# Gathers of batch n+2 between the scatters of batch n in the first layer's sums

## What is computed

```python
def spmm(edge_row, edge_col, edge_val, m):
    gathered = edge_val[:, None] * m[edge_col]
    return jax.ops.segment_sum(gathered, edge_row, num_segments=N_NODES)
h = spmm(edge_row, edge_col, edge_val, x @ W1)
h = jax.nn.relu(h)
out = spmm(edge_row, edge_col, edge_val, h @ W2)
...
x = _layernorm(x + _L0_gnn_ref(x, src, dst, edge_weight, L0_gnn_W1, L0_gnn_W2), axis=-1)
```

## Time and profile before

| what | value |
|---|---|
| median of 3 runs | 11682.42 us (11674.79 to 11685.21) |
| the profiled execution | 11694.18 us, its span 11692.3 us |
| mean granted TensorE clock of the span | 0.728 |
| PE busy, share of the span | 7181.3 us, 61% |
| PEld (weight loads) busy | 6410.3 us, 55% |
| VectorE (DVE) busy | 5776.1 us, 49% |
| ScalarE (ACT) busy | 2434.9 us, 21% |
| POOL busy | 6563.8 us, 56% |
| first and last gather (L1107) begin | 945.0 us, 4218.3 us |

### The profile page before, as it was taken

One profiled execution on the slowest core, in us unless ns is written; L12 is line 12 of the kernel. 1 busy time (PEld: TensorE's weight loads), 2 busy tenths in 40 slices (PEclk: granted clock), 3 DMA queues, 4 the chain that ended last, 5 costly groups with the idle time before them and its releaser, 6 DMA issues. The chain is left out here.

```text
span 11692.3 us, 252242 instructions
## 1 busy us (share of the span) xinstructions
PE 7181.3 (61%) x80158; PEld 6410.3 (55%) x80186; DVE 5776.1 (49%) x20072; ACT 2434.9 (21%) x6859; POOL 6563.8 (56%) x6504
## 2 busy tenths in 40 slices
PE   5877999977999966333333633333332466666663
PEld 5867998856988953333333433333331355555552
DVE  7985666635666663111111242222225466666665
ACT  3552222222222222000000000000001233333332
POOL 1324555524555523777777227777773377777771
PEclk8888999998999977555555565555555666666665
DMA  1015555545555544111111111111112111111113
GB/s 37 0 35 126 134 133 130 133 105 129 132 132 131 131 135 164 52 53 52 52 53 52 49 48 52 52 52 53 52 52 62 48 49 49 50 49 49 49 50 57
DMA packets 760187, 884.18 MB, mean 76 GB/s; under 512 B 136806, under 2 KB 645583, under 8 KB 760015
## 3 DMA queue, kind: packets, MB, share of 16 engines
q0 software_dynamic: 203776, 424.26, 15.7%
q1 hardware_dynamic: 555880, 452.87, 13.4%
q10 hardware_dynamic: 487, 6.55, 0.2%
HBM read 766.26 MB, written 123.29 MB: 76 GB/s over the span
## 5 line engine op out<-in xcount | busy, mean ns | idle before, releaser
L521 PE MATMUL psum<-sel,ring 128*128 128x128 f32 x6272 | 1451.3, 426 | 2533.6 <-DMA ring<-hyp_table,idx 1268.2
L521 PEld LDWEIGHTS psum<-sel,ring 128*128 128x128 f32 x6272 | 1356.3, 329 | 2629.2 <-issue 2629.2
L456 POOL DMA_INDIRECT ring<-att_table,idx x1592 | 1762.3, 1107 | 501.8 <-issue 472.1
L456 POOL DMA_INDIRECT ring<-hyp_table,idx x1568 | 1487.4, 949 | 487.2 <-issue 477.6
L456 POOL DMA_INDIRECT ring<-rel_table,idx x1568 | 1484.3, 947 | 487.0 <-issue 477.3
L508 DVE TENSOR_TENSOR acc<-acc,psum 128x128 f32 x392 | 113.1, 289 | 3075.2 <-PE psum L521 3075.2
L1107 PE MATMUL psum<-state,ring 128*128 128x128 bf16 x24420 | 1517.9, 221 | 40.8 <-DVE ring L1054 34.6
L1061 DVE TENSOR_SCALAR state<-iota_row,state 128x128 f32<-128x128 f32 x5684 | 1527.9, 346 | 0.0
L1107 PEld LDWEIGHTS psum<-state,ring 128*128 128x128 bf16 x24420 | 1380.0, 98 | 150.3 <-issue 51.5
L1040 POOL DMA_INDIRECT ring<-gcn_table,idx x812 | 781.3, 962 | 748.4 <-ACT idx L1085 624.7
L1040 POOL DMA_INDIRECT ring<-rows,idx x812 | 780.4, 961 | 742.3 <-ACT idx L1085 618.4
(11 more groups left out here) (353 smaller groups left out, 11153.5 us busy)
## 6 DMA issues: line engine op xcount, KB each, us to landing
state<-xparts SPq DMA_DIRECT2D x814, 192.0 KB
state<-drow SPq DMA_DIRECT2D x814, 160.0 KB
rel_table<-tout SPq DMA_DIRECT2D x98, 512.0 KB, 2.6
ring<-rows SPq DMA_DIRECT2D x70, 448.0 KB
ring<-att_table,idx POOLq DMA_INDIRECT x1592
ring<-rel_table,idx POOLq DMA_INDIRECT x1568
ring<-hyp_table,idx POOLq DMA_INDIRECT x1568
rows<-acc SPq DMA_DIRECT2D x42, 448.0 KB
```

Of the source, the lines that this page charges most:

```text
L456: pool.indirect_dma_start(out=ring[:, u, k, 0:width], out_offset=None, in_=table, in_offset=bass.IndirectOffsetOnAxis(ap=idx[:, u, k:k + 1 ...
L521: last = nc.tensor.matmul(psum[:, u % 2, 0:WIN], ring[:, u, k, 0:D], sel[:, u % 2, k, :], start=(k == 0), stop=(k == K - 1))
```

## The change

TensorE's loop body becomes one function, `step`. Where `gather` of batch n+1 with its 30 products stood ahead of `scatter` of batch n, the products that gather cell j of batch **n+2** now stand ahead of the scatters of cell j of batch n, for j = 0 to 4; cells 5 and 6 have scatters alone. Since n+2 and n have the same v, the buffers of a step are those of one parity. All the waits of the gathers, and that for `picked`, stand at the head of the step. VectorE makes the slots of n+2 ahead of the sources of n, and batches 0 and 1 are gathered ahead of the loop; SP loads one more batch at the end, whose gathers nobody uses. CT, the size of the table of places, stays the same number.

```diff
--- before.py
+++ after.py
@@ -49,7 +49,7 @@
 GB = -(-(-(-E // P)) // GC)
 assert GB % 2 == 0 and (GB + 1) * GC <= EC and AW * SW <= NPAD and AW <= P
 CELLS = SG * GB * SJ
-CT = -(-(CELLS + SJ) // P)
+CT = -(-(CELLS + 2 * SJ) // P)
 BC = SJ * P
 PC = JP * P
 TOP = TILES * P - SW
@@ -1025,9 +1025,11 @@
                         with sp.Fori(0, GB // 2) as it:
                             for v in range(2):
                                 load(sg * GB + it * 2 + v, it * 2 + v, v)
-                    load(LAST, GB, 0)
-                    sp.wait_ge(sem("xin0"), (LAST // 2 + 1) * 16)
-                    sp.wait_ge(sem("din0"), (LAST // 2 + 1) * 16)
+                    for v in range(2):
+                        load(LAST + v, GB, v)
+                    for v in range(2):
+                        sp.wait_ge(sem(f"xin{v}"), (LAST // 2 + 1) * 16)
+                        sp.wait_ge(sem(f"din{v}"), (LAST // 2 + 1) * 16)
 
                 @block.gpsimd
                 def _(pool):
@@ -1064,12 +1066,13 @@
                         ins.then_inc(sem("picked"), 1)
 
                     nc.vector.memset(zeros_b, 0.0).then_inc(sem("sent"), 1)
-                    to_slots(0, 0, 16)
+                    for v in range(2):
+                        to_slots(v, v, 16)
                     with dve.Fori(0, SG) as sg:
                         with dve.Fori(0, GB // 2) as it:
                             for v in range(2):
                                 n = sg * GB + it * 2 + v
-                                to_slots(n + 1, 1 - v, sg * (GB * 8) + it * 16 + (16 + 16 * v))
+                                to_slots(n + 2, v, sg * (GB * 8) + it * 16 + 32)
                                 to_sources(n, v)
                         dve.wait_ge(sem("closed"), sg + 1)
                         win = acc[:, bass.ds(sg * SUMS, SUMS)].rearrange("p (j h s) -> p j h s", h=2, s=P)
@@ -1097,23 +1100,28 @@
 
                 @block.tensor
                 def _(pe):
-                    def gather(n, v, loaded):
+                    def may_gather(n, v, loaded):
                         pe.wait_ge(sem("reach"), n + 3)
                         pe.wait_ge(sem(f"xin{v}"), loaded)
                         pe.wait_ge(sem("got"), n + 1)
-                        for j in range(JP):
-                            for t in range(2):
-                                for i in range(3):
-                                    last = nc.tensor.matmul(rowsP[v][:, j * P:(j + 1) * P],
-                                                            reach[v][:, t, j * P:(j + 1) * P],
-                                                            xwin[v][:, t, i, :],
-                                                            start=(t + i == 0), stop=(t + i == 3))
-                        last.then_inc(sem("gat"), 1)
-
-                    def scatter(n, v, fetches):
-                        pe.wait_ge(sem("got"), n + 3)
+
+                    def gather(v, j):
+                        for t in range(2):
+                            for i in range(3):
+                                last = nc.tensor.matmul(rowsP[v][:, j * P:(j + 1) * P],
+                                                        reach[v][:, t, j * P:(j + 1) * P],
+                                                        xwin[v][:, t, i, :],
+                                                        start=(t + i == 0), stop=(t + i == 3))
+                        if j == JP - 1:
+                            last.then_inc(sem("gat"), 1)
+
+                    def step(n, v, loaded, fetches):
+
+                        may_gather(n + 2, v, loaded)
                         pe.wait_ge(sem("picked"), n + 1)
                         for j in range(SJ):
+                            if j < JP:
+                                gather(v, j)
                             if j == JP:
                                 pe.wait_ge(sem(f"g{v}"), fetches)
                             rows = got[v][:, j * P:(j + 1) * P] if j < JP else fetched[v][:, j - JP, :]
@@ -1136,15 +1144,18 @@
                     pe.sem_inc(sem("scat"), 2)
                     pe.sem_inc(sem("reach"), 2)
                     pe.sem_inc(sem("got"), 2)
-                    gather(0, 0, 16)
+                    for v in range(2):
+                        may_gather(v, v, 16)
+                        for j in range(JP):
+                            gather(v, j)
                     with pe.Fori(0, SG) as sg:
                         pe.wait_ge(sem("sent"), sg + 1)
                         clear(True)
                         with pe.Fori(0, GB // 2) as it:
                             for v in range(2):
                                 n = sg * GB + it * 2 + v
-                                gather(n + 1, 1 - v, sg * (GB * 8) + it * 16 + (16 + 16 * v))
-                                scatter(n, v, sg * (GB // 2 * 16 * JQ) + it * (16 * JQ) + 16 * JQ)
+                                step(n, v, sg * (GB * 8) + it * 16 + 32,
+                                     sg * (GB // 2 * 16 * JQ) + it * (16 * JQ) + 16 * JQ)
                         clear(False)
             fence()
```

## The result

| | before | changed |
|---|---|---|
| median | 11683.81 us (4 runs) | 13077.0 us (13074.39 to 13081.27, 4 runs) |
| profiled execution | 11694.18 us | 13081.27 us, span 13079.5 us |
| mean granted TensorE clock | 0.728 | 0.752 |

The ratio is 1.1194, with a 95% interval of 1.1174 to 1.1213: the change makes the kernel **1393 us slower**. The forecast was 13000, the range 12580 to 13400.

What follows compares the result with a forecast made beforehand. TensorE's own work sets today's pace; after the change, the loop through DMA and VectorE would bind at 5.20 us a step. 1348 - 60 + 17 + 11 = +1316 us on 11694.18 gives 13010, forecast 13000 us, range 12580 to 13400.

Steps and rivals of the forecast that it cites:

- Turns: TensorE, between gathers and half-array scatters: four more turns a batch at 0.29 us, its own batch from 3.54 to 4.70 us.
- B: TensorE: short turns cost nothing, but the loop through DMA and VectorE binds at 4.63 us a step; 12540 us, chance 0.08.
- C: TensorE: half-array weights load beneath gathers, even today's turn disappears, step 3.25 us; 11420 us, chance 0.02.
- The loop: Gathers' end through SP, drow wait and VectorE to the gathers two steps on: 10.41 us, 5.20 us a step.
- Which binds: Loop through DMA and VectorE at 5.20 us a step, above TensorE's 4.70, so TensorE is late by 0.5 us.
- Rival A: Only the turns are paid: drow wait shrinks by over 1.0 us, TensorE binds at 4.70 us; 12590 us, chance 0.07.
- Size of the step: TensorE's loop, 812 steps: each grows from 3.54 to 5.20 us, +1348 us.
- small terms: Scatters' wait for fetched rows (25.4 us) goes, gathers' wait for VectorE (34.6 us) is inside the new loop: together -60 us.
- Boundaries: At 12 boundaries between groups, VectorE's L1061 now stands before TensorE's next gather: 12 x 1.4 = +17 us.
- The starts of the passes: First step of a pass now waits for batch 2's load: 2 x 5.6 = +11 us.
- Rival D: TensorE's clock: stalls and turns put a quarter of the time at the lower level, mean step 6.25 us; 13850 us, chance 0.08.

Runs made afterwards that it cites:

- the run with the sources first: Changed kernel, but VectorE makes the sources of batch n before it waits for the drow load of batch n+2: 12631.95 us, ratio 1.0807.
- Both ways of opening it: Changed kernel with VectorE's sources of n ahead of slots of n+2, 12631.95 us; or with SP's drow load ahead of its wait for the gathers, 12619.31 us.
- the loop alone: Changed kernel with cells not interleaved, 30 gathers then all scatters, wait for `picked` still ahead of the gathers: 12249.42 us, ratio 1.0479.
- three turns: Changed kernel with VectorE's sources ahead of its slots, and cells interleaved in twos instead of singly: 12230.64 us, ratio 1.0464.

## Why the prediction was right

- **Turns.** Taking the full price and not zero was right: the intervals of the earlier trace rows stand in every cell of the changed kernel, and the run with the sources first has steps of 4.76 us without a stall (4.70 predicted). That is 0.305 us a turn and not 0.29. The difference is the first gather behind a turn: in the changed kernel's trace it starts at 1506.186 and the next at 1506.253, 0.067 us instead of 0.056. The prediction's mean over 30 gathers hid it. The rule of the Trainium skill (TensorE: Matmul & The Clock Gate, section "Part 2: What happens when you issue a matmul"), that weight loads run ahead, does not reach across the change of mode here: the first half-array weights load together with their product (1505.76), and the third scatter comes 0.21 us behind the first in every cell, where 0.11 is the usual pace. Rivals B and C fall with it.
- **The loop.** 10.41 us for two steps, 10.45 in the steps shown, each term within 0.05 us. Both ways of opening it gave the time that TensorE alone allows.
- **Which binds.** The loop does, as forecast. The costs do not add: the turns alone (12632) are worth 945 us, the loop alone (12249) 563, together 1508, and the change lost 1393. Each hides part of the other. Rival A, turns alone, would have been 945 (its own sum said 910) of 1393.
- **Size of the step.** +1.66 us x 812 = 1348 us, measured 1.65 to 1.66, from 3.65 to 5.31. But the levels are both 0.11 us over mine (3.54 and 5.20), and here lies the term that failed, *small terms*, "together -60". The 3.65 could be read from the earlier trace rows (56 batches in 204.4 us); I took the steady 3.54 and gave back 60 us of waits. The waits did go, but the changed kernel is over its own level of 5.20 again. Of the 77 us by which the forecast was short, 52 are here and 19 in the boundaries below. Its loop, in the mean over 783 pairs of steps that cross no boundary, is 4.01 + 0.18 + 0.57 + 3.29 + 2.52 + 0.09 = 10.66 us: every term is a little over, the gathers' end most (4.01 against 3.90, with the steps at the lower clock in it), the drow wait by 0.05.
- **Boundaries.** Reckoned +17 us, measured 36. From the start of a group's last step to that of the fifth in the next group it is 34.6 us, 8.1 more than five steps of 5.30; before it was 23.4 us, 5.1 more than five of 3.65: 12 x 3.0 = 36. The later start was seen (1.0 us of it in the rows shown), the longer stretch at a clock of 0.50 was not. What each of the two is worth no run took apart. The starts of the passes, from the first gather to the loop's first, are 10.0 us against 4.1, so 2 x 5.9 = 12, forecast 11. With 812 x 1.65 = 1340 this makes 1388 of the 1393 us.
- **Rival D.** Within the groups the granted clock stood at 1.00 but for two stretches of 6.8 us, though TensorE stalled and turned. Its mechanism is there, but not for the quarter of the time that it needed.

## What to carry to other kernels

Products on the whole array and on half of it are better kept in long blocks of their own: a turn there and back costs 0.3 us here, as much as five bf16 products of 128 columns, and to interleave them cell by cell was the dearest order tried. When a buffer is filled for a step two ahead, write down the loop from its last reader through DMA, the engine behind it and the wait at the next step's head; what stands beside other work in the middle of a step comes into that loop as soon as its wait is moved to the head. And a loop with several links can be opened at the cheapest one: the order of two calls was worth 445 us here, the order of two DMA issues 458, and both opened the same loop.

## What the runs showed that was not expected

- Behind a boundary the granted clock was back at 1.00 after 3.4 us at 0.50 in the kernel before, and mostly after 10.2 us in the changed one, though TensorE was busy 10.11 of 10.20 us there by the profile. With three turns a step it was 6.8 us at ten of 12 boundaries. Work broken up by turns came back later to the higher level. But with one turn and the early wait for `picked` it was 6.8 us at eight of 12 as well, so turns are not all of it, and the cause is not shown.
- The same program took 11687 us on two chips and 13180 to 13280 us on three others, so times are compared by ratios to the kernel before on the same chip alone. Nothing of that shows ahead of the changed stage: the first gather starts at 945.0 us on a fast chip and at 947.7 and 947.1 us on two slow ones.
